# Gated cross-attention with a ternary feed-forward layer: 16-bit projections, a new order of the work, and one transposed attention result for two batches

## What is computed

```python
def _L0_xattn_ref(x, context, context_mask, Wq, Wk, Wv, Wo):
    q = (x @ Wq) ...        # 16 heads of 16
    k = (context @ Wk) ...
    v = (context @ Wv) ...
    scores = jnp.einsum('bhid,bhjd->bhij', q, k) * scale
    scores = jnp.where(context_mask[:, None, None, :], scores, max_neg)
    attn = jax.nn.softmax(scores, axis=-1)
    return einsum('bhij,bhjd->bhid', attn, v) ... @ Wo
x = x + jnp.tanh(g_xattn[0]) * _L0_xattn_ref(_layernorm(x), ctx_768, mask, Wq, Wk, Wv, Wo)
x = x + jnp.tanh(g_ffn[0]) * _L0_ffn_ref(_layernorm(x), W1, b1, W2, b2)   # ternary weights, exact gelu
```

## Time and profile before

| | |
|---|---|
| three runs | 1663.63, 1667.67, 1668.81 us (median 1667.67) |
| the profiled execution | 1664.17 us, span 1662.4 us |
| mean granted TensorE clock | 0.984 |
| PE, weight loads | busy 1508.0 us (91%), 1007.7 us (61%) |
| DVE | busy 1489.1 us (90%) |
| ACT | busy 939.8 us (57%) |
| POOL | busy 668.8 us (40%) |
| DMA | mean 71 GB/s |

### The profile page before, as it was taken

The page is one execution under the profiler, slowest core; times in us unless marked ns, Lnnn a source line. Parts: engine busy times, 40 slices in busy tenths (PEclk is TensorE's granted clock), DMA queues, the critical chain, the costliest instruction groups (busy, mean ns, idle before and its releaser), DMA issues.

```text
span 1662.4 us, 48262 instructions
## 1 busy us (share of the span) xinstructions
PE 1508.0 (91%) x14501; PEld 1007.7 (61%) x14501; DVE 1489.1 (90%) x4379; ACT 939.8 (57%) x1799; POOL 668.8 (40%) x813
## 2 busy tenths in 40 slices
PE   3899999999999999999999999987999999999998
PEld 2566666666666666666666666655666666666665
DVE  7799999999999999999999999987888888888886
ACT  2456666665656666565656566654555555555554
POOL 5354555455555545554555545552111111111111
PEclk9899999999999999999999999996999999999999
DMA  2333333333333333333333333321010110101101
GB/s 78 92 99 85 96 84 88 93 86 97 84 96 83 97 84 94 86 87 95 86 97 83 98 83 95 81 49 55 26 38 25 38 38 25 38 25 38 38 25 51
DMA packets 207471, 117.93 MB, mean 71 GB/s; under 512 B 24912, under 2 KB 207184, under 8 KB 207440
## 3 DMA queue, kind: packets, MB, share of 16 engines
q1 hardware_dynamic: 207440, 117.54, 26.2%
HBM read 32.53 MB, written 16.78 MB: 30 GB/s over the span
## 4 chain that ended last, share of the span: by engine, by line
PE 55%; DVE 26%; issue 13%; ACT 3%; DVEq 2%; ACTq 0%; DMA 0%
PE bank L1069 12%; PE bank L312 9%; PE bank L1098 5%; PE bank L1099 5%; DVE smax L751 5%; PE bank L336 5%; PE bank L319 4%; PE bank L303 4%; DVE rstd L691 3%; DVE xres L796 3%; DVE k L721 3%; PE bank L392 2%; DVE rstd L693 2%; DVE y L1056 2%; DVE rstd L684 2%
## 5 line engine op out<-in xcount | busy, mean ns | idle before, releaser
L924 POOL TENSOR_TENSOR probl<-prob 128x512 f16<-128x512 f32 x512 | 529.2, 1042 | 531.2 <-ACT prob L602 530.3
L602 ACT ACTIVATE prob<-bank,masks 128x512 f32<-128x512 f32 x512 | 345.4, 688 | 138.9 <-PE bank L371 138.9
L751 DVE TENSOR_REDUCE smax<-bank 128x4 f32<-128x512 f32 x512 | 348.2, 681 | 13.5 <-PE bank L336 9.7
L1085 DVE TENSOR_TENSOR hidl<-hid 128x512 f16<-128x512 f32 x256 | 226.0, 883 | 80.5 <-ACT hid L1080 79.7
L1080 ACT ACTIVATE hid<-bank,b_sb 128x512 f32<-128x512 f32 x256 | 176.1, 688 | 211.3 <-PE bank L1069 205.3
L1069 PE MATMUL bank<-y,w1T 128*128 128x512 f16 x1024 | 264.6, 381 | 29.2 <-DVE y L1056 28.0
L1163 POOL TENSOR_TENSOR xres<-xres,b2g 128x1024 f32 (+1 forms) x32 | 75.7, 2366 | 431.4 <-ACT yln L1033 413.5
L1098 PE MATMUL bank<-w2T,hid 128*128 128x256 f16 x1024 | 237.4, 273 | 0.6 <-ACT w2T L1013 0.6
L1099 PE MATMUL bank<-w2T,hidl 128*128 128x256 f16 x1024 | 237.4, 273 | 0.0
L336 PE MATMUL bank<-k_rows,q_rows 64*128 64x128 f16 x2048 | 226.8, 220 | 5.6 <-DMA q_rows<-smaxT 3.4
L371 PE MATMUL bank<-q_rows,k_rows 64*128 64x128 f16 x2048 | 201.7, 219 | 0.8 <-DMA q_rows<-smaxT 0.8
(11 more groups left out here) (92 smaller groups left out, 2555.7 us busy)
## 6 DMA issues: line engine op xcount, KB each, us to landing
q_rows<-q SPq DMA_DIRECT2D x512, 64.0 KB, 2.5
k_rows<-k SPq DMA_DIRECT2D x512, 64.0 KB, 2.5
xres<-in_x_dram SPq DMA_DIRECT2D x64, 256.0 KB, 2.7
out_dram<-ystage SPq DMA_DIRECT2D x32, 512.0 KB, 2.9
ctx_sb<-in_ctx_dram SPq DMA_DIRECT2D x64, 192.0 KB, 3.2
q_rows<-smaxT SPq DMA_DIRECT2D x128, 8.0 KB
w_raw<-in_L_ffn_W_dram SPq DMA_DIRECT2D x2, 1024.0 KB, 7.0
prob<-in_L_xattn_Wq_dram SPq DMA_DIRECT2D x1, 256.0 KB, 4.2
```

The source lines that it names most:

```text
L602: act.activation(prob[u][:], st_bank[u % 2][:], ACT.Exp, bias=0.0, scale=masks[g.parity][:, 2 + b:3 + b]).then_inc(exp_done, 1)
L751: dve.tensor_reduce(smax[:, b, u * UH:(u + 1) * UH], sm_bank[u % 2][:].rearrange("p (h j) -> p h j", h=UH), AX.X, ALU.max).then_inc(max_ta ...
L924: pool.tensor_tensor(probl[u][:], prob[u][:], prob[u][:].bitcast(BF16)[:, 1::2], ALU.subtract).then_inc(prob_split, 1)
```

## The change

It does nine things, all in the attention stage and its start.

1. The three input projections and the output projection use 16-bit parts: three matmuls (`SPLIT`: high by high, high by low, low by high) in place of each 32-bit one. The weights are split once at the start, scaled by 64 (`high_weights` on ACT, `low_weights` on DVE); the context's 192 columns are two pieces of 96.
2. x and the context are split in place by POOL (`low_x`, `low_ctx`) and transposed in 16 bits: eight transposes in place of four, and one copy of 128x1024 16-bit elements.
3. The low part of `prob` is written by POOL into the low halves of `prob` itself; the tiles `probl` go, and k has two tiles (`k16`).
4. The attention result is transposed, projected and added once for a group, both batches together, one group late; DVE makes its low part (`low_attn`), new.
5. The maxima are transposed into `pv_bank[0]`, no longer into `tr_bank`.
6. `read_weighed` writes its sums into PSUM, and `normalise` reads them there.
7. Layer normalisation of x is done for four batches at once, in every second group. DVE only does the statistics and the seed (`seed_x`, 4 parts); the Newton steps go to POOL (`root_x`, 14 small operations).
8. q, k and v are in `pj_bank` in an order that lets one instruction read all 512 columns.
9. The order of all five lists is new.

The core of the diff:

```diff
-            for k in range(KD):
-                last = pe.matmul(pj_bank[:, m * T:(m + 1) * T], wq_sb[:, k, m * P:(m + 1) * P],
-                                 xlnT[:, k, :], start=(k == 0), stop=(k == KD - 1))
+            for k in range(KD):
+                for i, (wp, xp) in enumerate(SPLIT):
+                    last = pe.matmul(by_batch(m), wq16[:, wp, k, m * P:(m + 1) * P],
+                                     typed(xT16[:, xp, k, :], xp).rearrange("p (b s) -> p b s", b=2),
...
+        def transpose_max(pe, g, b):
+            n = g.batch(b)
+            pe.wait_ge(max_split, n + 1)
+            if not (isinstance(n, int) and n < 2):
+                pe.wait_ge(norm_done, 2 * n - 3)
+            pe.transpose(pv_bank[0][0:2 * HEADS, 0:S // 2].bitcast(F16), smax16[:, b, :],
...
         def pe_group(pe, g, left):
...
+            scores(pe, g, 0, 0, (g, 1, 3))
+            if not first:
+                weigh(pe, before, 1, 2)
+            if left >= 2:
+                pe.wait_ge(v_split, g.n + 1)
+                project_q(pe, g2, 0)
+            scores(pe, g, 0, 1, (g1, 0, 0) if left >= 1 else None)
+            if not first:
+                weigh(pe, before, 1, 3)
+            transpose_max(pe, g, 1)
+            if left >= 2:
+                project_q(pe, g2, 1)
+                tr = transpose_ctx(pe, g2, tr)
+            scores(pe, g, 0, 2, (g1, 0, 1) if left >= 1 else None)
+            pe.wait_ge(maxT_copied, g.batch(0) + 2)
+            weigh(pe, g, 0, 0)
+            scores(pe, g, 0, 3, (g1, 0, 2) if left >= 1 else None)
+            weigh(pe, g, 0, 1)
+            if not first:
+                tr = transpose_attn(pe, before, tr)
+            if left >= 2:
+                pe.wait_ge(q_split, g.n + 3)
+                project_k(pe, g2, 0)
+            scores(pe, g, 1, 0, (g1, 0, 3) if left >= 1 else None)
+            weigh(pe, g, 0, 2)
+            if left >= 2:
+                project_k(pe, g2, 1)
+            scores(pe, g, 1, 1, (g1, 1, 0) if left >= 1 else None)
+            weigh(pe, g, 0, 3)
+            if left >= 1:
+                transpose_max(pe, g1, 0)
+                if left >= 2:
+                    pe.wait_ge(k_split, g.n + 3)
+                project_v(pe, g1, 0)
+            scores(pe, g, 1, 2, (g1, 1, 1) if left >= 1 else None)
+            if left >= 1:
+                pe.wait_ge(maxT_copied, g.batch(1) + 2)
+            weigh(pe, g, 1, 0)
+            if left >= 1:
+                project_v(pe, g1, 1)
+            if left >= 3:
+                tr = transpose_x(pe, g.after(3), tr)
+            scores(pe, g, 1, 3, (g1, 1, 2) if left >= 1 else None)
+            weigh(pe, g, 1, 1)
+            if not first:
+                tr = project_out(pe, before, tr)
...
         def act_group(act, g, left):
...
             exponentials(act, g, 0, 0)
             exponentials(act, g, 0, 1)
+            copy_maxT(act, g, 1)
+            if left >= 2:
+                high_q(act, g2)
+                copy_ctxT(act, g2)
             exponentials(act, g, 0, 2)
             exponentials(act, g, 0, 3)
             if not first:
+                copy_attnT(act, before)
             exponentials(act, g, 1, 0)
+            if left >= 2:
+                high_k(act, g2)
             exponentials(act, g, 1, 1)
+            if left >= 1:
+                copy_maxT(act, g1, 0)
             exponentials(act, g, 1, 2)
+            if left >= 1:
+                high_v(act, g1)
+            if left >= 3:
+                copy_xT(act, g3)
             exponentials(act, g, 1, 3)
+            if left >= 4:
+                apply_x(act, g4)
...
+        def low_attn(dve, g):
+            dve.wait_ge(attnT_high, g.n + 1)
+            dve.tensor_tensor(attnT16[:, 1].rearrange("p k t -> p (k t)"), tr_bank[:],
+                              attnT16[:, 0].rearrange("p k t -> p (k t)"), ALU.subtract).then_inc(attnT_split, 1)
...
         def add_attention(dve, g):
+            dve.wait_ge(projected, g.n + 1)
+            rows = xres[:, bass.ds(g.batch(0), 2), :]
+            dve.scalar_tensor_tensor(rows, tr_bank[:].rearrange("p (b d) -> p b d", b=2), gate_xw, rows, ALU.mult,
+                                     ALU.add).then_inc(x1_done, 1)
```

More of the change, by code:

```diff
@@ L317, in project_v @@
         def project_v(pe, g, b):
-            for k, rows in enumerate((P, C1)):
-                last = pe.matmul(pj_bank[:, b * D:(b + 1) * D], ctxT[g.parity][0:rows, k, b * S:(b + 1) * S],
-                                 wv_sb[0:rows, k, :], start=(k == 0), stop=(k == 1))
+            for k in range(2):
+                for i, (wp, xp) in enumerate(SPLIT):
+                    last = pe.matmul(pj_bank[:, b * D:(b + 1) * D],
+                                     typed(ctxT16[g.parity][:, xp, k, b * S:(b + 1) * S], xp),
+                                     wv16[:, wp, k, :], start=(k == 0 and i == 0 and b == 0),
+                                     stop=(k == 1 and i == 2), skip_group_check=True)
             if b == 1:
@@ L450, in pe_first @@
             project_k(pe, g1, 1)
-            transpose_max(pe, g0, 0, tr)
-            for u in range(2):
+            transpose_max(pe, g0, 0)
+            for u in range(3):
                 rough_scores(pe, g0, 1, u)
@@ L460, in pe_group @@
             before, g1, g2 = g.after(-1), g.after(1), g.after(2)
-            tr = [(maxT_copied, 1)] if first else []
-            scores(pe, g, 0, 0, (g, 1, 2))
+            if first:
+                tr = [(xT_copied, 3)]
+            elif isinstance(g.half, int) and g.n == 1:
+                tr = [(xT_copied, 4)]
+            else:
+                tr = [(x1_done, g.n - 1)]
+            scores(pe, g, 0, 0, (g, 1, 3))
             if not first:
                 weigh(pe, before, 1, 2)
-                tr = project_out(pe, g.batch(0) - 2, tr)
-            scores(pe, g, 0, 1, (g, 1, 3))
-            if not first:
-                weigh(pe, before, 1, 3)
             if left >= 2:
@@ L865, in dve_group @@
+                if g.parity == 1 and left >= 6 and i < SEED_PARTS:
+                    seed_x(dve, g.half + 3, i)
+            before = g.after(-1)
+            if not first:
+                read_weighed(dve, g.batch(0) - 1, 1, 0)
+                norm(0)
+                normalise(dve, before, 1, 0)
+            else:
+                norm(0)
             take_max(dve, g, 1, 3)
             round_max(dve, g, 1)
-            norm(10)
+            norm(1)
             low_max(dve, g, 1)
+            norm(2)
@@ L869, in dve_group @@
+            if left >= 1:
+                take_max(dve, g1, 0, 0)
+            norm(3)
+            if left >= 2:
+                low_q(dve, g2)
+            if left >= 1:
+                take_max(dve, g1, 0, 1)
+            norm(4)
             if not first:
                 read_weighed(dve, g.batch(0) - 1, 1, 1)
[L871 to L877 removed]
@@ L878, in dve_group @@
-            norm(13)
-            if left >= 1:
-                take_max(dve, g1, 0, 1)
-            read_weighed(dve, g.batch(0), 0, 0)
-            normalise(dve, g.batch(0), 0, 0)
+                norm(5)
+                normalise(dve, before, 1, 1)
+            else:
+                norm(5)
             if left >= 1:
                 take_max(dve, g1, 0, 2)
-            if left >= 2:
-                low_k(dve, g2)
-            if not first:
-                add_attention(dve, g.batch(0) - 1)
+            norm(6)
@@ L890, in dve_group @@
+            read_weighed(dve, g.batch(0), 0, 0)
+            norm(7)
+            normalise(dve, g, 0, 0)
             if left >= 1:
@@ L1238, in _ @@
             pick_masks(pool, Group(0, 0))
-            over_groups(pool, pool_group)
+            low_x(pool, Group(0, 1))
+            low_ctx(pool, Group(1, 0))
+            low_x(pool, Group(1, 0))
+            for i in range(8):
+                root_x(pool, 2, i)
+            over_groups(pool, pool_group, 3)
             pool.wait_ge(b2_scaled, 1)
```

557 lines of the change are left out of this document (323 added, 234 removed).

## The result

The changed kernel takes **1792.95 us** (median of 4 runs, 1790.05 to 1798.21) against 1667.27 of the kernel before: ratio 1.0761, 95% interval 1.073 to 1.0792. It is slower, as forecast, but by 126 us and not by 35; 1793 lies well above the range of 1630 to 1745. The profiled execution took 1790.05 us.

A forecast was written before the change was run, and what follows sets the result against it. The prediction took a closed loop of waits across PE, ACT and DVE, averaging 17.35 us a group, as the bound: 1664.2 + 24 (loop) + 12 (`low_max` waiting for POOL) + 2 (start) = 1702 us, range 1630 to 1745.

The forecast's parts named there:

- The loop: Waits from `low_max` of batch 1 through q, k, v and `project_out` back: 16.56 us, 18.13 with statistics, average 17.35; +24 us.
- the wait of `low_max` for POOL: In slot 5, `low_max` of next batch 0 may wait behind `low_prob`: 0.2 of 0.8 us a group put in, +12 us.
- the lower of the two prices: Named error in the loop: `high_q` and `high_k` at 0.59 instead of 0.69 us would take 0.2 us off.
- the statistics: In every second group, four statistics add 1.23 us before step 4's division, and copy and aggregations 0.34.
- Busy time: Work per group on each engine: PE some 12.4 us, DVE 13.1, POOL 12.4, all below the old period of 16.96.
- rival A: A loop step does not hold, so DVE's sum decides: 14.7 us a group, 1524 us, faster; chance 0.10.
- rival C: `low_max` loses against POOL nearly always: 18.15 us a group, 1740 us; chance 0.20.
- rival D: Granted clock falls to 0.95 as PE has gaps; PE's part of the loop grows 0.4 us, about 1727 us; chance 0.05.
- the start: Splitting weights on ACT and DVE, with Newton steps no longer behind POOL's clearing: +2 us, between -5 and +8.

The follow-up runs named there:

- two of the filled ones: Changed kernel with next batch 0's maxima behind k, and the kernel with four moves, each with unread matmuls in TensorE's gaps: 1690.95 and 1607.99 us.
- the move of the maxima: Changed kernel with `round_max` and `low_max` of next batch 0 behind `low_attn` and `low_k`, half `project_v` and slot 7 ahead of `transpose_max`: 1717.35 us.
- the filled gaps: Changed kernel with unread 512-column matmuls in all four TensorE gaps, 3 (11 in groups with statistics), 3, 3 and 3: 1763.94 us.
- the kernel with four moves: Changed kernel with x loaded early, batch 0's maxima behind k, x's transposes and copy in TensorE's gap, and q ahead of batch 1's maxima: 1871.89 us.

## Why the prediction was right or wrong

**Which steps failed.** The loop was read rightly. What failed are the two terms put on top of it: the wait of `low_max` for POOL, put in at 0.2 us a group, measured at about 1.06; and the clock, put in at 0, measured at 0.9 to 1.0. With the first alone taken away the kernel takes 1717 us, inside the range of 1630 to 1745; with the second alone, 1764, outside it.

**The closed loop: right, its close agreement partly luck.** Its terms as measured, with the forecast in brackets: half a projection 0.82 (0.82), `high_q` and `high_k` 0.60 (0.69), `low_q` to the next start 0.61 (0.67), `copy_xT` 1.01 (1.01), `project_out` 1.48 (1.48). The kernel with both other causes taken away has 17.29 us a group where 17.35 was worked out. But its odd groups hold a wait for the load of x, 0.3 to 0.8 us each, that the forecast left out. Without it, even groups are 16.35 (16.56) and odd ones 17.62 (18.13), 16.99 on average: the loop was put 0.36 too high, and the missing wait hid it. That `high_q` has the lower of the two prices was named as an error; the statistics cost 1.85 in the pair shown, with their load's wait of 0.46, and 1.27 with the load early (17.62 less 16.35), where 1.57 was put in.

**Busy time: right.** At full clock (the pair from 566.3) PE does 12.8 us a group, DVE 13.8, POOL 11.9, where 12.4, 13.1 and 12.4 were worked out; the excess of DVE is covered by the waiting inside `low_max` and `round_max`. That no engine is near its limit didn't help: rival A was rightly held to be unlikely.

**The wait of `low_max` for POOL: the mechanism right, the size wrong.** It was put in at 0.2 of 0.8 because the two starts were closer than my error. POOL comes first in every group (rival C), so `low_max` takes 0.96 to 1.02 us each time, and `round_max`, for which I allowed nothing, is held up too, by 0.36 in every second group. Added up from the durations that is 1.0 us a group; from the periods it is 18.05 - 16.99 = 1.06. Rival C had put the period at 18.15, and the pair at full clock has 18.05: with a chance of 0.20 it was the better forecast. The Trainium skill, SBUF — State Buffer, section Who interferes with whom, lists `tensor_scalar` too among the instructions that can need the shared pair of ports, in a 2-port mode; the runs agree (0.53 for `round_max` beside POOL, 0.17 alone), and a `tensor_reduce` in the place of `low_max` took 0.19 beside POOL, as that section says it would.

**The clock (rival D): a term put at nothing.** It had a chance of 0.05, a clock of 0.95 and 0.4 us, with the remark that no row shows what happens at 71% busy. It was 0.89 in the stage and 19.04 - 18.05 = 0.99 us a group, of which about 0.1 is the wait for the load of x. So the price for a given fall of the clock was about right, and the fall itself was missed. The remark was true, and that was the reason to give the case more than 0.05 and not less: the rows of before were all at 93% busy and said nothing on either side.

**The whole.** Between the changed kernel and two of the filled ones (19.04, 17.29 and 15.83 us a group; 1790, 1691 and 1608 us) a microsecond of the period is worth about 57 us. With 57, the 126 us are: the loop 0.03 x 57 = 2 (24 predicted), the waits for POOL 60 (12), the clock with the late load 56 (0), and some 8 (2) that stay for the start, the first and last groups and weren't taken apart. These shares come from periods and depend on the order in which the causes are taken away. By the runs, the move of the maxima is worth 73 to 76 us and the filled gaps 26 to 29, or up to 40 with what the added matmuls cost: less waiting for POOL also meant less time at the lower clock. By runs as by periods, the wait for POOL is the larger of the two.

The late load of x, which the prediction left out, is a wait of 0.4 to 0.6 us in 6 of the 17 odd groups looked at in the changed kernel; alone, its removal gave 13 us.

## What to carry to other kernels

When a change takes work off TensorE and leaves the period to a loop of waits, ask first what its share of idle time will be: this kernel went from 93% busy to 71% at full clock (25.59 of 36.10 us) and lost 2 to 3% to the clock, and several reorderings that made single groups shorter gained little, as the clock fell with them. Before a reordering is judged, run it once with unread matmuls in TensorE's gaps; here that turned a verdict of 12% slower into 3.5% faster. And on VectorE, a tiny instruction on a loop can cost what GpSimd's long one costs when it starts a moment later (`low_max`: 0.17 us alone, 1.01 behind an operation of 1.04). In a kernel that repeats itself this came out the same way in every group, so count it in full: put the instruction where GpSimd has no long operation under way.

## What the runs showed of the hardware

In the kernel with four moves TensorE's longest waits are 0.7 to 1.2 us, and the granted clock was at half for some 13 of 20 us in every group. In the changed kernel it fell at about 606.2 us (0.59 between 606 and 607), within a wait of 2.9 us, and stayed at half for about 7 us, to 613.0. That gaps are what brings it down is shown by filling them; a wait of 2.28 us (568.1 to 570.4) passed at a clock of 1.00. Half a projection takes 0.82 us at 2.4 GHz and 1.46 at 1.2, four 32-bit transposes 0.66 and 1.12, 12 matmuls of `project_out` 1.48 and 2.59. Which gap does it isn't settled: in some odd groups of the changed kernel it fell and in others of the same order it did not. The Trainium skill, TensorE: Matmul & The Clock Gate, section Part 1, describes the half rate as the default, which recent activity releases; the runs agree, since activity alone, with results nobody reads, gave the full clock back.
